# An attention and feed-forward kernel: the inverse transform in tiles of 64x32, and a new order of the first steps, the last pairs and the weight maxima

## The reference, cut to what matters

```python
# x, ctx: (128, 128, 256) float32; 16 heads of 16 columns
def attention(q_in, kv_in):                      # q_in = layernorm(x)
    Q, K, V = (a @ w as (batch, head, dim, time) for each)
    corr = irfft(rfft(Q) * conj(rfft(K)), n=L)   # along time, L = 128
    top_vals, top_idx = top_k(corr, 4)           # floor(log(128)) = 4
    w = softmax(top_vals)
    out = sum_i w[i] * (V rolled along the head's 16 columns by top_idx[i])
    return out @ wo
def feed_forward(x):                             # 256 -> 1024 -> 256
    W_in, W_out quantized to 8 bits per column / row by their maxima
    x and hidden quantized to 16 bits by their global maxima
    return quantize16(gelu(x @ W_in + b_in)) @ W_out + b_out
x = x + attention(layernorm(x), ctx)
x = x + feed_forward(layernorm(x))
```

## Time and profile before

| | |
|---|---|
| runs | 1050.58, 1053.34, 1055.65 us; median 1053.34 |
| profiled execution | 1052.56 us, its span 1050.7 |
| TensorE busy | 1020.9 us, 97% of the span |
| VectorE busy | 985.4 us, 94% |
| ScalarE busy | 885.6 us, 84% |
| GpSimd busy | 516.1 us, 49% |
| attention half | up to 579.06 us |

### The profile page before, as it was taken

One profiled execution on the slowest core, in us unless ns is written; L12 is line 12 of the kernel. 1 busy time (PEld: TensorE's weight loads), 2 busy tenths in 40 slices (PEclk: granted clock), 3 DMA queues, 4 the chain that ended last, 5 costly groups with the idle time before them and its releaser, 6 DMA issues. The chain is left out here.

```text
span 1050.7 us, 30275 instructions
## 1 busy us (share of the span) xinstructions
PE 1020.9 (97%) x9870; PEld 763.5 (73%) x9870; DVE 985.4 (94%) x2838; ACT 885.6 (84%) x1569; POOL 516.1 (49%) x742
## 2 busy tenths in 40 slices
PE   6899999999999999999988999999999999999998
PEld 5788888888888888888866444444444888888887
DVE  4899999999999999999978999999997999999998
ACT  4578787888888888888867788888888999999996
POOL 6799888998999999999965300000001000000000
PEclk9999999999999999999998999999999999999999
DMA  5345444343345444444421598999989999999995
GB/s 174 117 159 164 147 127 138 120 148 125 130 144 150 131 131 129 137 150 142 129 75 52 172 326 305 318 305 298 296 305 365 346 359 350 362 349 358 351 354 198
DMA packets 145111, 226.82 MB, mean 216 GB/s; under 512 B 76256, under 2 KB 87520, under 8 KB 140896
## 3 DMA queue, kind: packets, MB, share of 16 engines
q1 hardware_dynamic: 143600, 224.00, 62.7%
q10 hardware_dynamic: 1392, 1.31, 0.4%
HBM read 121.26 MB, written 83.89 MB: 195 GB/s over the span
## 5 line engine op out<-in xcount | busy, mean ns | idle before, releaser
L671 PE MATMUL sums<-wout,arena 128*128 128x256 f16 x2048 | 229.7, 273 | 1.2 <-DVE arena L1552 1.2
L671 PEld LDWEIGHTS sums<-wout,arena 128*128 128x128 f16 x2048 | 197.0, 98 | 32.4 <-DVE arena L1545 7.3
L1552 DVE SCALAR_TENSOR_TENSOR arena<-arena,wout_rel 128x512 f16<-128x512 int16 x256 | 180.3, 745 | 2.0 <-ACT arena L942 0.9
L640 PE MATMUL sums<-arena,win 128*128 128x512 f16 x512 | 115.9, 379 | 0.7 <-DVE arena L1497 0.7
L640 PE MATMUL bank<-arena,win 128*128 128x512 f16 x512 | 115.7, 379 | 0.0
L1516 DVE TENSOR_REDUCE hmax_all<-arena 128x1 f32<-128x1024 f32 x96 | 111.3, 1211 | 2.9 <-ACT arena L899 2.9
L1113 POOL CAST store_x<-one 128x1 bf16<-128x1 f32 x1 | 0.2, 193 | 218.8 <-DVE one L1534 218.8
L942 ACT ACTIVATE arena<-arena,wout_rel 128x512 f16<-128x512 int16 x159 | 106.2, 706 | 0.0
L899 ACT ACTIVATE arena<-sums,b_in_sb,z_scale 128x512 f32<-128x512 f32 x128 | 97.5, 778 | 9.7 <-PE sums L640 5.1
L935 ACT ACTIVATE arena<-arena,one 128x1536 int16<-128x1536 f32 x63 | 99.2, 1575 | 4.5 <-DVE arena L1552 3.0
L491 PE MATMUL sums<-store_x,arena 128*128 128x256 f16 x768 | 94.2, 272 | 2.8 <-ACT arena L691 2.8
(11 more groups left out here) (152 smaller groups left out, 2376.3 us busy)
## 6 DMA issues: line engine op xcount, KB each, us to landing
hidden_scratch<-arena SPq DMA_DIRECT2D x32, 1536.0 KB, 5.5
arena<-hidden_scratch SPq DMA_DIRECT2D x64, 768.0 KB, 6.7
arena<-in_ctx_turned SPq DMA_DIRECT2D x64, 256.0 KB, 2.9
arena<-in_x_turned SPq DMA_DIRECT2D x64, 256.0 KB, 3.2
arena<-in_x SPq DMA_DIRECT2D x64, 256.0 KB, 3.6
x_scratch<-arena SPq DMA_DIRECT2D x64, 256.0 KB, 3.4
arena<-x_scratch SPq DMA_DIRECT2D x32, 512.0 KB, 5.8
out<-arena SPq DMA_DIRECT2D x31, 512.0 KB, 4.3
```

The costliest lines, as they stand in the source:

```text
L640: last = nc.tensor.matmul(bank[f][:, :].rearrange("p (n t) -> p n t", n=4), win16[:, f, c, :], xt[q % 3][:, s, :, c, :], start=s == 0 and ...
L671: last = nc.tensor.matmul(bank[m * 2 + k // 2][:, k % 2 * D:(k % 2 + 1) * D], gbuf[:, s, f, k * P:(k + 1) * P], wout16[:, f, :], start=f = ...
L1552: V.scalar_tensor_tensor(gbuf[:, 1, f, :], hq[:, f, :], wout_rel[:, f:f + 1], gbuf[:, 0, f, :], ALU.mult, ALU.subtract).then_inc(S["c_lo"], 1)
```

## The change

It changes the shape of the inverse transform's matmuls and the places of existing operations in the engines' lists. No operation of the computation is added or dropped, apart from the way in which pairs 59 and 60 get their second layer norm's sums (BY_BN from 5 to 3). BY_HAND goes from 5 to 4. FILL = 3 marks the first steps that have an order of their own.

```diff
-W_LOAD = 4
+W_LOAD = 2
-BY_BN = 5
-BY_HAND = 5
+BY_BN = 3
+BY_HAND = 4
+FILL = 3
...
 # SyncE
+            def load_wo():
+                sp.wait_ge(S["w_split"], 1)
+                for n, k in ((2, 0), (3, 1)):
+                    for part in (slice(0, NF), slice(NF, P)):
+                        sp.dma_start(w_attn_raw[part, n, :, :], ...).then_inc(s_w_in[2], 16)
...
                 load_x(t + 1)
+                if t == 0:
+                    load_wo()
...
-                c = 2 * (t - W_LOAD)
-                if 0 <= c < FC:
+                for c in (4 * (t - W_LOAD), 4 * (t - W_LOAD) + 2):
+                    if 0 <= c < FC:
...
             for t in range(PAIRS - 1):
                 step(t)
+            spread_blocks(PAIRS - 5)
             load_x_turned(PAIRS - 1)
...
 # TensorE, inverse
-                            last = nc.tensor.matmul(bank[5 + b][:, e * P:(e + 1) * P], csum[half_of, k, e * P:(e + 1) * P],
-                                                    inv32[half_of, k, :], start=k == 0, stop=k == 1)
+                            for strip in range(4):
+                                last = nc.tensor.matmul(bank[5 + b][strip * 32:strip * 32 + 32, e * P:(e + 1) * P], csum[half_of, k, e * P + strip * 32:e * P + strip * 32 + 32],
+                                                        inv32[half_of, k, :], start=k == 0, stop=k == 1)
...
                     project_k(t)
-                    project_v(t)
-                    project_q(t)
+                    if 0 < t < FILL:
+                        project_q(t)
+                        project_v(t)
+                    else:
+                        project_v(t)
+                        project_q(t)
...
 # ScalarE
+                if 1 < t <= FILL:
+                    take_q_half(t - 1)
                 if active(t, 1):
                     take_v(t - 1)
...
-                if active(t, 1):
+                if active(t, 1) and not 1 < t <= FILL:
                     take_q_half(t - 1)
...
-                if t == 0:
-                    load_wo()
...
             take_k(PAIRS - 1)
-            spread_blocks(PAIRS - 5)
             normalize2(PAIRS - 8)
             take_q_half(PAIRS - 1)
             squares(PAIRS - 6)
-            exponent(PAIRS - 3)
-            normalize2(PAIRS - 7)
             high_ot(PAIRS - 5)
             take_ot(PAIRS - 5)
             take_q(PAIRS - 1)
+            exponent(PAIRS - 3)
+            normalize2(PAIRS - 7)
             spread_blocks(PAIRS - 4)
...
             take_ot(PAIRS - 3)
+            squares(PAIRS - 5)
             spread_blocks(PAIRS - 2)
-            normalize2(PAIRS - 5)
             high_ot(PAIRS - 2)
             take_ot(PAIRS - 2)
+            normalize2(PAIRS - 5)
+            squares(PAIRS - 4)
             spread_blocks(PAIRS - 1)
-            normalize2(PAIRS - 4)
             high_ot(PAIRS - 1)
             take_ot(PAIRS - 1)
+            normalize2(PAIRS - 4)
             normalize2(PAIRS - 3)
...
 # GpSimd
+                if t < FILL:
+                    scale_both(t - 7)
+                    if active(t, 1):
+                        low_xt(t - 1)
                 if active(t, 0) and t > 0:
                     mix_ct(t)
-                if active(t, 1):
+                if active(t, 1) and t >= FILL:
                     low_xt(t - 1)
...
-            scale_both(PAIRS - 5)
+            minus_mean2(PAIRS - 5)
             take_shift(PAIRS - 1)
             low_ot(PAIRS - 3)
+            scale_both(PAIRS - 5)
+            minus_mean2(PAIRS - 4)
+            low_ot(PAIRS - 2)
             scale_both(PAIRS - 4)
-            low_ot(PAIRS - 2)
+            low_ot(PAIRS - 1)
             scale_both(PAIRS - 3)
-            low_ot(PAIRS - 1)
             scale_both(PAIRS - 2)
...
 # VectorE, weights(t)
+                if 4 <= t < 6:
+                    for k in range(4):
+                        largest_w(w_in_raw, win_max, (t - 4) * 4 + k, "win_chain")
+                if t == 6:
+                    floor_w(win_max, "win_chain")
+                    dve.wait_ge(S["w_out_in"], 16 * FC // 2)
+                    for k in range(2):
+                        largest_w(w_out_raw, wout_max, k, "wout_chain")
+                if t == 7:
+                    invert_w(win_max, win_up, "win_chain")
+                if t == 8:
+                    scale_w(win_up, "win_chain").then_inc(S["w_in_scaled"], 1)
+                m = (t - W_STEP) // 2 + 2
+                if t % 2 == 0 and 2 <= m < FC:
+                    largest_w(w_out_raw, wout_max, m, "wout_chain")
...
 # VectorE
+                if t < FILL:
+                    statistics1(t)
+                    moments1(t)
                 if active(t, 1):
                     mix_q(t - 1)
...
             head_lags(PAIRS - 4)
+            mix_q(PAIRS - 2)
             one_hot(PAIRS - 4)
...
             mask_sum(PAIRS - 4)
-            mix_q(PAIRS - 2)
...
             products(PAIRS - 2)
+            magnitude(PAIRS - 8)
             top_values(PAIRS - 3)
             mix_q(PAIRS - 1)
-            magnitude(PAIRS - 8)
...
             one_hot(PAIRS - 3)
+            products(PAIRS - 1)
...
-            products(PAIRS - 1)
             top_values(PAIRS - 2)
...
-            statistics2(PAIRS - 5)
-            moments2(PAIRS - 5)
-            statistics2(PAIRS - 4)
-            moments2(PAIRS - 4)
...
+            magnitude(PAIRS - 7)
             residual(PAIRS - 3)
             statistics2(PAIRS - 3)
             moments2(PAIRS - 3)
-            magnitude(PAIRS - 7)
             magnitude(PAIRS - 6)
             magnitude(PAIRS - 5)
             magnitude(PAIRS - 4)
             residual(PAIRS - 2)
```

More of the change, by code:

```diff
@@ L248, in xattn_ffn_kernel @@
             c_hi_dve c_lo c_f c_out first_int y_inverse bias_chain bias_ready kp_done kf_out w2_done
-            rsum_chain mt_zero half_ready center w_mean w_centred w_in_i w_in_staged w_out_scaled
+            rsum_chain mt_zero half_ready win_chain wout_chain center w_mean w_centred w_in_i w_in_staged w_out_scaled
             w_out_i wout_ready qp_done qf_out xt_high xt_ready ln_pow scales_done bt_done
-            turned_early early_out w_scale_chain""".split()
+            turned_early early_out""".split()
         S = {n: sem("s_" + n) for n in names}
@@ L341, in store_x1 @@
                 sp.dma_start(x1_v[p], x1[p % 2].rearrange("p b d -> p (b d)")).then_inc(s_x1_st[p % 2], 16)
+            def load_wo():
+                sp.wait_ge(S["w_split"], 1)
+                for n, k in ((2, 0), (3, 1)):
+                    for part in (slice(0, NF), slice(NF, P)):
+                        sp.dma_start(w_attn_raw[part, n, :, :], wo.rearrange("(c k p) n -> k p c n", c=DC, k=2)[k]).then_inc(s_w_in[2], 16)
             load_turned(0)
@@ L698, in _ @@
             load_w(1, wv)
[L700 to L704, removed]
             def high_w(n):
@@ L1056, in step @@
                     take_shift(t - 3)
-                scale_both(t - 7)
+                if t >= FILL:
+                    scale_both(t - 7)
                 if active(t, 2):
@@ L1125, in _, with largest_w, floor_w, invert_w @@
             V = nc.vector
-            def largest_w(raw, top_, k):
-                V.tensor_reduce(top_[:, k:k + 1], raw[:, k, :], AX_X, ALU.max, apply_absolute_value=True).then_inc(S["w_scale_chain"], 1)
-            def floor_w(top_, done):
-                dve.wait_ge(S["w_scale_chain"], done)
-                V.tensor_scalar(top_[:, :], top_[:, :], TINY, None, ALU.max).then_inc(S["w_scale_chain"], 1)
-            def invert_w(top_, up, done):
-                dve.wait_ge(S["w_scale_chain"], done)
-                V.reciprocal(up[:, :], top_[:, :]).then_inc(S["w_scale_chain"], 1)
-            def scale_w(up, done):
-                dve.wait_ge(S["w_scale_chain"], done)
+            def largest_w(raw, top_, k, chain):
+                V.tensor_reduce(top_[:, k:k + 1], raw[:, k, :], AX_X, ALU.max, apply_absolute_value=True).then_inc(S[chain], 1)
+            def floor_w(top_, chain):
+                dve.wait_ge(S[chain], FC)
+                V.tensor_scalar(top_[:, :], top_[:, :], TINY, None, ALU.max).then_inc(S[chain], 1)
+            def invert_w(top_, up, chain):
+                dve.wait_ge(S[chain], FC + 1)
+                V.reciprocal(up[:, :], top_[:, :]).then_inc(S[chain], 1)
+            def scale_w(up, chain):
+                dve.wait_ge(S[chain], FC + 2)
                 return V.tensor_scalar(up[:, :], up[:, :], INT8, None, ALU.mult)
@@ L1165, in weights @@
             def weights(t):
[L1167 to L1168 removed]
+                if t == 4:
                     dve.wait_ge(S["w_in_loaded"], 16 * FC // 2)
[L1170 to L1188 removed]
+                if 4 <= t < 6:
[3 more added lines that the diff above has]
+                    floor_w(win_max, "win_chain")
+                    dve.wait_ge(S["w_out_in"], 16 * FC // 2)
+                    for k in range(2):
[7 more added lines that the diff above has]
```

(9 more changed lines are left out.)

30 lines of the change are left out of this document (5 added, 25 removed).

## The result

The changed kernel takes 1061.22 us (median of 6 runs, 1060.04 to 1063.04), the kernel before beside it 1054.48: a ratio of 1.0074, interval 1.0059 to 1.0089. It is 6.7 us slower; 1046 was forecast, and the time lies outside the range. The profiled execution took 1063.04 us, its span 1061.2, which is 10.5 more than the span before. (That is more than the 6.7 of the medians, since the profiled execution is the slowest of the six here, while the one before, 1052.56, is one of the faster ones.)

What follows compares the result with a forecast made beforehand. VectorE at 8.31 us a step, only 0.05 under TensorE, was taken to limit the gain. From 1052.56, less 5.0 (middle) and 4.2 (first steps), plus 2.5 (last pairs): 1046 us, own range 1043 to 1048.5, 8 in 10 1041 to 1053.

Steps and rivals of the forecast that it cites:

- Inverse in 64x32 tiles: Inverse transform in the attention steps: smaller tiles take 0.2 us off TensorE's step, from 8.36 to 8.15.
- rival 1: Small tiles are bound by instruction issue: inverse 1.95 us, step 9.1, kernel 1092 us, slower; chance 7%.
- issue is not what spaces the rounds: Transform matmuls: a round's eight records start in two groups 0.02 us apart, so rounds of half the columns take 0.11.
- The middle: The 58 attention steps between first steps and last pairs: 491.8 us becomes 486.9, -5.0.
- a stall not thought of: Anywhere in the kernel: an unforeseen stall makes it slower than before; no size, chance 3%.
- the moved maxima: Weight maxima moved partly to steps 4 to 6, where VectorE has room: about 2 us of the middle's gain.
- the 0.05 us a step: Middle steps: VectorE's 8.31 lets only 0.05 us of TensorE's gain per plain step be cashed; about 3 us in all.
- First steps: Start of the attention half: earlier project_q(0), q before v, and full clock give -4.2 us, between -5.0 and -2.4.
- Last pairs: End of the attention half: the new order costs +2.5 us, between +1.0 and +4.0.
- the low clock: Last pairs: TensorE's idle times bring a low-clock stretch again, nothing to 3 us, taken as 1.5.
- the place of normalize2(60) and scale_both(61): Last pairs: standing behind take_ot and low_ot(63), they delay magnitude and last_residual, +1.0 us.
- spread_blocks(63) comes only about 1 us sooner: Last pairs: two squares of 1.1 us each, ahead of spread_blocks(62) and (63) on ScalarE, limit the gain to 1 us.

Runs made afterwards that it cites:

- run 6: The kernel of run 5 with the inverse in 64x32 tiles and long satisfied waits added to TensorE's list to move the fetch border: 1048.05 us, 0.995.
- run 7: The kernel of run 5 with the inverse in tiles of 64x64: 1046.10 us, 0.9937 of the kernel before.
- run 1: The changed kernel with its inverse back in tiles of 64x128, all new orders kept: 1051.92 us, 0.9984 of the kernel before.
- run 5: The kernel before with only the new first steps and moved weight maxima; old inverse and old last pairs: 1047.67 us, 0.9938.
- run 12: The changed kernel with the inverse in tiles of 64x64 and both last-pairs repairs of run 11: 1047.16 us, 0.9948 of the kernel before.
- run 9: The kernel of run 1 with VectorE's statistics again for pairs 59 and 60 in place of ScalarE's squares: 1049.91 us, 0.9958.
- run 11: The kernel of run 9 with normalize2(60) ahead of high_ot(63) and scale_both(61) ahead of low_ot(63) again: 1048.41 us, 0.9952.
- run 2: The kernel before with nothing changed but the inverse in tiles of 64x32: 1059.67 us, 1.0059.
- run 3: The changed kernel with long satisfied waits added, putting the fetch border 125 instructions into the inverse every fourth step: 1070.50 us, 1.0161.

## Why the prediction was wrong, by its own steps

**Inverse in 64x32 tiles: right about the array, wrong about what feeds it.** Eight rounds, begun 0.2 us behind the transform, and 1.09 us up to project_k: as forecast. 64 records in 1.09 us are 17 ns apiece, so rival 1 falls. The rule of about 25 ns that it cited from the Trainium skill (TensorE: Matmul & The Clock Gate, "Wait — 56ns, not 53.3ns?") does not hold in this trace for tiles side by side. MAX8 to MAX8 is 8.30 to 8.32 in undisturbed steps, as forecast. The sentence "issue is not what spaces the rounds" is true of the rounds. The step that failed is what was built on it: TensorE's step was put at 8.15 in all 58 steps, and nothing was put down for bringing in 6144 more instructions. In six steps TensorE ran out of them and stood for 1.3 to 1.7 us. The forecast had terms for the engines and for the DMAs that carry data, but none for the queue that carries the program, which stands in the same table of the profile.

**The middle: -5.0 forecast, +8.4 measured.** The six breaks are 8.7 us of idle time by the waits. By the stretch they cost more, with what follows them and the smaller waits: 10.1 us against run 6, which has the same tiles (500.20 less 490.09), and 11.6 against run 7 (488.61). The forecast's chance for a stall not thought of was 3%, without a size. Without the breaks the middle gains 2.2 to 3.2 (runs 1, 5, 7 and 12; 1.5 in runs 9 and 11, where a wait of project_q(39) for ScalarE stands in it), not 5.0. Of that the moved maxima give 2.4 (run 5, old inverse), where 2 was put down, and the tiles, as 64x64, about 0.8 (488.61 against 489.40), not 3. So the second term that was wrong is the 0.05 us a step in all 58 steps. The gain in pace is there only where TensorE set the step, in 28 of them: 233.20 us in run 7 against 234.03 before. From step 10 to 34 the time is 203.41 us in run 7 and 203.42 in run 5 (92.15 to 295.57): VectorE sets those steps, with small tiles or large.

**First steps: -4.2 forecast, -3.5 measured.** Project_q(0) starts at 11.28, forecast near 11.3, and the whole first stretch is at a granted clock of 1.00, where the earlier trace rows has 0.96, with 3.4 us of it at 0.51. x_turned(1) lands earlier too (ScalarE takes it at 15.17 instead of 16.79). Without the small tiles the stretch takes 39.7 to 40.9 us; where the last tenths lie was not taken apart. The two rows that answer to the earlier trace rows, from the timeline of the first step:

```profile
11.28 1.49 PE L501 MATMUL sums<-store_x,arena 128*128 128x256 f16 x12 [0.78 <-DVE store_x L1174]
...
15.17 0.63 ACT L706 ACTIVATE arena<-arena 128x512 f16<-128x512 f32 x1 [1.90 <-DMA arena<-in_x_turned]
```

**Last pairs: +2.5 forecast, +5.3 measured.** Two terms were priced, and both are there: the low clock (0.53 around attend(62), which takes 2.02 us instead of 1.16), and the place of normalize2(60) and scale_both(61), worth 2.6 alone and 1.5 on top of the other repair, where 1.0 was put down. The step that failed is "spread_blocks(63) comes only about 1 us sooner". Counted from project_k(62), it comes at 36.1 us instead of 32.8. The forecast saw the squares as a replacement for a normalize2 of equal length, but normalize2(59) did not go: it moved out of the time of attend(62) to a place behind take_ot(62), together with squares(60). There the two hold spread_blocks(63) back by 2.0 us, and TensorE stands for 1.60 us of it before attend(63). That the wait before turn_weights(60) goes and that transform(62) and (63) come 1.1 and 1.8 us sooner (run 1) was right (1.4 and 2 were forecast). But attend(61) was to come about 3 us sooner and came 0.3 sooner (26.2 us from project_k(62) against 26.5 before; 1.1 in run 1), and at attend(62) nothing is left: 30.8 us against 30.5.

**What stays open.** How many instructions ahead the next block is asked for, and so which places of the border are dangerous, is not settled. With tiles of 64x32 a border 122 to 127 instructions into an inverse that stands right behind a transform broke all 26 times in runs 2 and 3 and the changed kernel; one at 99 came twice and broke once; at 152 and 156 there were two waits of 0.4 us; at 157 and at 159, 15 times each, a wait of over 1 us came once each. Why a packet sometimes starts late wasn't tried; the trace shows when a packet moves, not when it is asked for.

## What to carry to other kernels

Count instructions as well as columns: when a tile is cut into smaller ones, look in the table of DMA queues at the instruction queue of the engine, work out how many instructions one packet holds, and compare the densest run of instructions with the time a packet needs. A slow step that comes back at a fixed number of steps, with a wait that nothing released, is the sign; a few idle instructions in the list move it and so prove it. In a hand-written order, ask of each instruction that is moved not how long it is but whose waiting time it used to fill, and what stands behind it now.

## What the runs showed of the hardware that was not expected

TensorE's instructions arrive in packets of 16,384 bytes, 256 instructions, each 0.9 to 1.9 us long in the traces; where they came too late at the end of an inverse, TensorE went on 2.2 to 2.7 us after the packet's start. 192 short instructions in 1.8 us ahead of a border are enough to run out of them.

Wait instructions on a semaphore long signalled follow each other every 0.11 us. 42 of them left TensorE idle for 2.57 us, and the stretch behind was granted 0.51 for 3.4 us; 7 a step, behind a projection of 1.3 us, cost nothing that can be seen.

Tiles side by side start close together: 64 records of 128 columns take 1.09 us to the next matmul, 17 ns each. As a whole the inverse is no faster for it: 16 records of 64x128 take 1.09 us too, and 32 of 64x64 take 1.04. An inverse of 64x64 behind a transform of 64x32 starts 0.33 us after its last round, one of the same shape 0.2.
